# Both transposes of a head pair in one run behind the value product, through one shared bank

## The reference

```python
q = jnp.einsum('btc,hdc->bhtd', x, Wq)
k = jnp.einsum('btc,hdc->bhtd', x, Wk)
...
v = jnp.einsum('bthe,bted->bhtd', mix_v, proj_v)
scores = jnp.einsum('bhid,bhjd->bhij', q * scale, k)
probs = jax.nn.softmax(scores, axis=-1)
attn = jnp.einsum('bhij,bhjd->bihd', probs, v)
...
res = jnp.einsum('bthe,bthd,efd->bthf', mask_o, attn, Wo)
return res.sum(axis=2)
```

## Time and profile before

| what | value |
|---|---|
| runs before | 2786.41, 2810.72, 2819.38 us; median 2810.72 |
| span of the profiled execution, first to last instruction | 2794.2 us |
| own time of the profiled execution | not listed apart from its span |
| mean granted TensorE clock | 0.940 |
| PE busy | 2408.3 us, 86% |
| DVE busy | 1489.2 us, 53% |
| ACT busy | 1376.4 us, 49% |
| POOL busy | 797.8 us, 29% |

### The profile page before, as it was taken

The page is one execution under the profiler, slowest core; times in us unless marked ns, Lnnn a source line. Parts: engine busy times, 40 slices in busy tenths (PEclk is TensorE's granted clock), DMA queues, the critical chain, the costliest instruction groups (busy, mean ns, idle before and its releaser), DMA issues. The chain is left out here.

```text
span 2794.2 us, 41667 instructions
## 1 busy us (share of the span) xinstructions
PE 2408.3 (86%) x15724; PEld 1368.8 (49%) x15724; DVE 1489.2 (53%) x2621; ACT 1376.4 (49%) x2944; POOL 797.8 (29%) x373
## 2 busy tenths in 40 slices
PE   3887798889898898988988898988989888987597
PEld 2344345554455444554455544554445543554465
DVE  4332674357734575436844576345754457336843
ACT  0334345653465544654466534765446532654274
POOL 1000580006700274004800166002730039004600
PEclk7996898999999998999989999999989999898799
DMA  2110110012000220003101130002200031000101
GB/s 82 41 64 1 30 47 1 27 51 69 27 16 17 66 65 12 16 24 88 46 1 31 46 73 23 16 16 66 64 12 16 16 88 46 1 16 24 34 25 42
DMA packets 210689, 101.15 MB, mean 36 GB/s; under 512 B 137367, under 2 KB 189620, under 8 KB 210492
## 3 DMA queue, kind: packets, MB, share of 16 engines
q1 hardware_dynamic: 205052, 95.74, 12.7%
q10 hardware_dynamic: 5440, 2.75, 0.4%
HBM read 77.48 MB, written 20.99 MB: 35 GB/s over the span
## 5 line engine op out<-in xcount | busy, mean ns | idle before, releaser
L789 POOL TENSOR_TENSOR prod<-pv,mixv 128x1024 f32<-128x1024 f32 x218 | 639.8, 2969 | 143.1 <-DVE vals L1623 106.2
L1660 DVE TENSOR_REDUCE nmax<-bank 128x1 f32<-128x512 f32 x512 | 339.4, 685 | 415.5 <-PE bank L1101 413.4
L1309 ACT ACTIVATE pr<-bank,nmax 128x512 f32<-128x512 f32 x512 | 352.3, 688 | 408.1 <-DVE nmax L1660 402.5
L729 POOL TENSOR_TENSOR rstd<-vareps,minus_half 128x4 f32<-128x4 f32 x48 | 49.4, 1029 | 1462.1 <-DVE vareps L1414 1462.1
L804 PE MATMUL bank<-ident,pr 128*128 128x128 f32 x2048 | 341.4, 291 | 90.3 <-ACT prT L1326 84.0
L804 PEld LDWEIGHTS bank<-ident,pr 128*128 128x128 f32 x2048 | 225.1, 145 | 352.0 <-issue 238.1
L1206 ACT ACTIVATE arena<-bank 128x512 f32<-128x512 f32 x256 | 152.9, 597 | 416.5 <-PE bank L920 394.4
L1326 ACT ACTIVATE prT<-bank 128x512 f32<-128x512 f32 x512 | 304.7, 595 | 26.5 <-PE bank L804 20.8
L1623 DVE TENSOR_REDUCE vals<-prod 128x128 f32<-128x1024 f32 x224 | 269.2, 1209 | 69.2 <-POOL prod L789 69.0
L920 PE MATMUL bank<-h1T,Wg 128*128 128x512 f32 x512 | 269.5, 608 | 18.0 <-ACT arena L1206 15.1
L928 PE MATMUL bank<-arena,Wd 128*128 128x512 f32 x512 | 265.7, 603 | 21.1 <-DVE arena L1511 21.1
(11 more groups left out here) (239 smaller groups left out, 3017.9 us busy)
## 6 DMA issues: line engine op xcount, KB each, us to landing
Wg<-in_L_ffn_Wg SPq DMA_DIRECT2D x64, 256.0 KB, 2.7
Wu<-in_L_ffn_Wu SPq DMA_DIRECT2D x64, 256.0 KB, 3.1
Wd<-in_L_ffn_Wd SPq DMA_DIRECT2D x64, 256.0 KB, 3.7
out_rows<-on SPq DMA_DIRECT2D x32, 512.0 KB, 2.6
onR<-out_rows SPq DMA_DIRECT2D x32, 512.0 KB, 4.1
xin<-in_L_attn_x SPq DMA_DIRECT2D x8, 256.0 KB, 5.3
mask_rows<-masko SPq DMA_DIRECT2D x8, 256.0 KB, 4.3
maskR<-mask_rows SPq DMA_DIRECT2D x8, 256.0 KB, 7.2
```

Of the source, the lines that this page charges most:

```text
L789: g.tensor_tensor(*value_piece(n), ALU.mult).then_inc(vprod_r[0], 1)
L1309: s.activation(pr[:, x % NPR, :], S[x % len(S)][:, :], ACT.Exp, bias=nmax[:, x % NPR:x % NPR + 1], accum_out=den[:, i % 2, h:h + 1]).then_ ...
L1660: v.tensor_reduce(nmax[:, m % NPR:m % NPR + 1], S[m % len(S)][:, :], X_AXIS, ALU.max, negate=True).then_inc(nmax_r[0], 1)
```

## The change

Only PE's program is changed. The transposes of units x-2 and x-1 both stand in the step of the even unit x, behind the scores of x and x+1 and behind the value product of x-4 and x-3. In the step of the odd unit x+1 PE has nothing left to do. The list of users of the shared bank is made in the same new order, by a new function `turned_at`. The other engines' programs are as before.

```diff
+def turned_at(k):
+
+    m = HEAD_OF[k] - 2
+    return (m, m + 1) if m % 2 == 0 and 0 <= m < N2 else ()
+
 TB_USES = [use for k, step in enumerate(HEAD_STEPS)
-           for use in ([step] if step in EXTRA_AT else []) + ([("head", lagging(k, 2))] if lagging(k, 2) is not None else [])]
+           for use in ([step] if step in EXTRA_AT else []) + [("head", m) for m in turned_at(k)]]
...
-                    m = lagging(k, 2)
-                    if m is not None:
-                        wait(pe, pr_r, b, m + 1)
-                        free_for(b, ("head", m))
-                        transposes(TP[m % len(TP)], lambda j: pr[:, m % NPR, j * P:(j + 1) * P]).then_inc(p_T[0], 1)
                     m = lagging(k, 3)
                     if m is not None and m % 2:
                         i, h = m // HS, m % HS
...
                         if h % GROUP == GROUP - 1:
                             last.then_inc(o_ps[0], 1)
+                    for m in turned_at(k):
+                        wait(pe, pr_r, b, m + 1)
+                        free_for(b, ("head", m))
+                        transposes(TP[m % len(TP)], lambda j: pr[:, m % NPR, j * P:(j + 1) * P]).then_inc(p_T[0], 1)
```

## The result

| | kernel before | changed kernel |
|---|---|---|
| median of 4 runs | 2807.12 us | 2977.74 us (2967.20 to 2982.83) |
| span of the profiled execution | 2794.2 us | 2971.5 us (its own time 2973.76) |
| mean granted clock | 0.940 | 0.922 |

The ratio of the runs is 1.0645 (95% interval 1.0605 to 1.0684; the two medians alone give 1.061): 6% slower. The forecast was 2952 us with a range of 2870 to 3025, so the time lies inside it.

The account below looks back on a forecast made before the run. PE's program order was taken to bound the head stages, through stands inside head pairs. Terms of 29 + 106 + 6 = 141 us on the 2810.7 us median gave 2952 us, 5% slower, range 2870 to 3025.

Parts of the forecast that it names:

- Kind A: One-bank head-stage pairs whose odd transposes already waited for the even copy: 0.21 us more each, 136 pairs, 29 us.
- Kind B: One-bank head-stage pairs that did not wait before: 0.84 to 1.43 us more each, taken as 1.2, 88 pairs, 106 us.
- The last stage, 6 us: Last head stage, two transpose banks: the value product now waits for the odd copy; 6 us, bounds 0 and 15.
- The ring: Last head stage: value product, transposes, copy, pr and odd copy form a 3.61 us cycle, where a pair took 3.26.
- the one change of array shape saved: Per pair on PE, three shape changes instead of four: 0.10 us each, up to 26 us off, counted as nothing.
- the third rival: Clock falls with the new gaps in the seven one-bank head stages: 98 us more, 3050 us; chance 15%.
- the sign set for it: What would show the clock falling: the head stages' granted clock is 0.90 or less.
- the 141 of the sum: Whole kernel: 29 us for pairs that waited, 106 for those that did not, 6 for the last stage.
- The first two rivals: Head stages: extras' waits vanish as copies finish sooner, 2795 us, 4%; or the cost is mostly swallowed, 2846 us, 11%.

Follow-up runs that it names:

- e6: The kernel before, with a head stage's side work allowed only behind odd steps: 2790.73 us, ratio 1.0008 to the kernel before.
- e5: The changed kernel, with a head stage's side work allowed only behind odd steps: 2836.36 us, ratio 1.0172 to the kernel before.
- e3: The changed kernel plus six unread identity transposes between even and odd transposes in the seven one-bank stages: 2927.34 us, ratio 1.0475 to the kernel before.
- e8: e5 plus six unread identity transposes in the wait between even and odd transposes: 2811.00 us, ratio 1.0051 to the kernel before.
- e7: e6 with the even units' prT copies made by VectorE instead of ScalarE: 2802.39 us, ratio 1.0041 to the kernel before.

## Why the prediction was right or wrong

*The direction and the mechanism* were right: the one bank, and the cover that both moves took from the copy. 224 waits were forecast and 224 came, 0.83 us each (0.7 to 0.8 forecast) and 186.9 us in all (170).

*Kind A, 0.21 us a pair:* 0.22 in the row above (3.52 against 3.30), and 0.20 by e6 against e5. Right.

*Kind B, 0.84 to 1.43:* the pair of the earlier trace rows was worked out at 1.43 and lost 7.93 - 6.54 = 1.39 up to its extra. That the order behind PE is the reason, ScalarE's above all, is shown by e5, which changes it and leaves PE's. The mean of 1.2 was about right: e3, with nearly the clock of before (153 us at the lower level in these stages, 159 before), has the seven stages at 1594.5 us, 117 more than before, of which 136 pairs at 0.17 (0.22 less the sooner start of 0.05) take 23; the other 94 in 88 pairs would be 1.07 each.

*The last stage, 6 us:* +3.4. The ring held in full only where ScalarE also copies `oaT`, as in the second pair below: 3.89 us from scores to scores (2851.06 to 2854.95), with a wait of 0.71 of the value product for the odd copy, where 3.61 plus 0.26 for `oaT` was worked out. Of 11 pairs without an extra, three were like this. Two took 3.52 us, and six 3.11 to 3.17 without that wait (2847.95 to 2851.06 is one), less than the 3.26 of before, where 3.61 was forecast for each.

```profile
2847.95 1.13 PE L1107 MATMUL bank<-keys_odd,qs 64*128 64x512 f32 x4
...
2851.06 1.13 PE L1107 MATMUL bank<-keys_odd,qs 64*128 64x512 f32 x4
...
2852.15 0.61 ACT L1331 ACTIVATE prT<-bank 128x512 f32<-128x512 f32 x1
...
2852.90 1.09 PE L1138 MATMUL bank<-prT,arena 128*64 128x128 f32 x16 [0.71 <-ACT prT L1331]
...
2853.93 1.09 PE L810 MATMUL bank<-ident,pr 128*128 128x128 f32 x8
...
2854.95 1.13 PE L1107 MATMUL bank<-keys_odd,qs 64*128 64x512 f32 x4
```

What I had not counted is that pairs in which nothing waits became 0.15 us faster each: 3.26 to 3.11, 3.69 to 3.54 with L1111, 4.15 to 4.00 with L1125. The two runs of transposes now stand together and take 1.02 us to the next scores (2853.93 to 2854.95), where each took 0.59 before; 0.10 was worked out from the earlier trace rows for the one change of array shape saved. The rule of the Trainium skill, "TensorEngine Tiling (Array Packing)", Key Properties, that a switch of mode drains the engine, agrees with these pairs (0.15 us less with one switch less). In the 224 others the saving stood in front of the wait, as argued.

*The term left out, the clock:* 167 us came in the seven stages where A and B were to bring 135. The step that failed is the one in the third rival, "gaps of 0.56 in most pairs left the clock at 0.97", by which I left the clock out of the sum. It fell, to 0.94 in the second stage. The time at the lower level rose from 335 to 464 us, and 92 of these 129 us lie in the seven stages. Two figures price it: PE is busy for 54.5 us more with the same instructions (a rough price, since the order alone moves the busy time as well: e5, with about the clock of before, has 2373.2 us, 35 less), and e3 brought some 37 us back through the clock (48 less at most 11 for the sooner start). That is about half of the 98 us that this rival gave it; the sign set for it, a clock of 0.90 or less, came in the seventh stage alone (0.84). PE's standing still grew by 122.8 us, less than the 141 of the sum. So one part of the sum was too high and another was missing, and that 2952 came so near is in part luck.

The profile shows one place where the clock fell, in the pair ahead of 871 and at the same point of each of the first six head stages:

```profile
862.44 0.63 PE L810 MATMUL bank<-ident,pr 128*128 128x128 f32 x4 [0.78 <-ACT prT L1331]
...
867.42 1.16 PE L1096 MATMUL bank<-hdB,WqT 128*128 128x128 f32 x8 [1.68 <-ACT prT L1331]
...
868.51 2.00 PE L966 MATMUL bank<-arena,attT 32*128 32x512 f32 x4
...
871.40 2.08 PE L1107 MATMUL bank<-keys_odd,qs 64*128 64x512 f32 x4
```

Products of this shape took 1.13 us in the kernel before, and the scores 1.13:

```profile
845.24 1.13 PE L960 MATMUL bank<-arena,attT 32*128 32x512 f32 x4
```

Here L966 takes 2.00 us and the scores 2.08. Ahead of it PE had waited 0.78 us for the even copy, and then 1.68 us for the odd one. The same place in e3, where the first of these waits is filled:

```profile
861.40 0.85 PE L1146 MATMUL bank<-ident 128*128 128x128 f32 x6
...
867.03 1.18 PE L1096 MATMUL bank<-hdB,WqT 128*128 128x128 f32 x8 [1.68 <-ACT prT L1335]
...
868.14 2.08 PE L966 MATMUL bank<-arena,attT 32*128 32x512 f32 x4
```

The level falls all the same, so at this place it falls behind the wait for the odd copy, which the side work makes long, with or without the other wait. In e5 the wait for the even copy is there and the long one is not; the products take 1.13 us (at 845.42), and the clock of the run is that of the kernel before. So the number of waits does not do it alone. What e3's filling took away is a fall in another place: at 991 in the changed kernel PE had stood for 0.78, 0.78 and 0.77 us within seven us, and the next scores (993.34) took 2.08 us; in e3 the first two are filled, and the same scores (991.45) take 1.13. What exactly a stand must be for the level to fall, these runs leave open. The rule weighed ahead (the Trainium skill, "TensorE: Matmul & The Clock Gate", A second HAM failure mode: small stands between groups of matmuls let the clock swing) agrees with e3 and e8, where filling such stands raised the clock; e5, with 224 of them at 0.942, speaks against it if it is read as a rule for any such stand.

*The first two rivals:* the extras' waits did not shrink (37.9 and 28.4 us), and nothing was swallowed.

No version was measurably faster than the kernel before; e6 equals it.

## What to carry to other kernels

Before work is moved out from between two users of one buffer, name what it covered, and follow the moved work on every in-order engine, not only on the one where it is moved: here the wait itself cost 0.2 us a pair, and the side work that it pushed back, standing on ScalarE ahead of the next copy, cost most of the rest, about half of it through the clock (e5). The row of one wait is a poor price, since a wait can move to another row: in e6 the transposes wait 65 us more and the extras 52 less, at no cost, and in e7 97 us leave the row while PE's standing still falls by 11 as a whole. Only between e6 and e5, where the extras' waits stay as they are, do row and time agree (46 us each). So add up the engine's idle and busy time as well. When PE gets new stands, put its clock into the sum, as a term and not as a rival.

## What I had not expected of the hardware

Useless work made the kernel faster: six transposes per pair, read by nobody, in a wait that had to be waited anyway, gained 1.7% in e3 and 1.2% in e8, by less time at the lower clock (464 to 363 us and 329 to 281 us). And the order with one change of tile shape less on PE is worth 0.15 us in a pair where nothing waits, not the 0.10 of two single rows.
